# Second layer of a graph network: logits, maxima and aggregation run as one stage over blocks of 20 steps, in place of three stages

## The reference

```python
x = x * rsqrt(mean(x*x) + EPS) * rms_w @ W_down          # 3125 x 256, H = 4 heads of D = 64
xl = (x @ Wl).reshape(n, H, D);  xr = (x @ Wr).reshape(n, H, D)
msg = xl[src] + xr[dst]                                   # per edge, and one loop per node
e = einsum('ehd,hd->eh', leaky_relu(msg, 0.2), att)
m = segment_max(e, dst)
p = exp(e - m[dst]);  denom = segment_sum(p, dst)
out = segment_sum(p / (denom[dst] + 1e-16) * xl[src], dst) @ W_up
```

## Time and profile before

| what | value |
|---|---|
| median of 3 runs | 2532.44 us (2525.97 to 2538.17) |
| profiled execution: span, first to last instruction | 2193.8 us |
| profiled execution: its own total time | not recorded beside the span; the median lies 338.6 us above the span |
| busy, share of the span | PE 83%, DVE 69%, POOL 55%, ACT 45% |
| PE granted clock, mean | 0.95 |
| DMA | 537 MB, mean 245 GB/s |
| node stage, logits, between, aggregation, last stage | 217, 539, 30, 188.6, 109.2 us |

### The profile page before, as it was taken

How to read it: one execution, slowest core, us unless ns; L and a number is a source line. 1 busy time by engine, 2 the same in 40 slices (tenths; PEclk the granted TensorE clock), 3 DMA queues, 4 the chain that set the end, 5 groups by cost and what they waited for, 6 DMA issues and landing times. The chain is left out here.

```text
span 2193.8 us, 51473 instructions
## 1 busy us (share of the span) xinstructions
PE 1812.9 (83%) x12059; PEld 1247.6 (57%) x12060; DVE 1515.3 (69%) x3657; ACT 997.4 (45%) x3133; POOL 1196.8 (55%) x1696
## 2 busy tenths in 40 slices
PE   4899999995888888888849896887878878577788
PEld 3555555543566656665638774666666666456643
DVE  6577777747666666666669983554656556888867
ACT  3200000024777777777747662332333333566566
POOL 1122222223777777777711116777777776688780
PEclk9999999997999999999979998998999999698899
DMA  8344553313999999999999965887878877998657
GB/s 332 112 108 106 105 106 109 99 44 120 364 357 355 362 357 356 356 359 353 361 260 321 308 199 166 238 245 212 252 224 253 240 217 225 291 332 307 231 193 261
DMA packets 254654, 537.42 MB, mean 245 GB/s; under 512 B 40301, under 2 KB 146422, under 8 KB 254510
## 3 DMA queue, kind: packets, MB, share of 16 engines
q0 software_dynamic: 87696, 275.50, 36.7%
q1 hardware_dynamic: 72670, 174.80, 24.8%
q10 hardware_dynamic: 94176, 85.76, 13.6%
HBM read 447.61 MB, written 101.28 MB: 250 GB/s over the span
## 5 line engine op out<-in xcount | busy, mean ns | idle before, releaser
L1248 ACT ACTIVATE wone<-onehot,w 128x64 f32<-128x64 f32 x1760 | 432.3, 334 | 148.1 <-DVE onehot L1294 143.2
L161 POOL DMA_INDIRECT acc<-xl_table,csrc x392 | 395.8, 1010 | 127.3 <-issue 113.0
L1265 PE MATMUL banks<-w_sb,wone 128*64 128x256 f32 x2368 | 315.9, 392 | 80.5 <-DMA w_sb<-xp_table,isrc 54.8
L161 POOL DMA_INDIRECT w_sb<-xp_table,isrc x296 | 296.1, 1000 | 90.6 <-issue 55.5
L973 PE MATMUL banks<-w_sb,acc 128*128 128x512 f32 x736 | 342.6, 604 | 0.0
L1290 DVE TENSOR_TENSOR acc<-banks,acc 128x512 f32 x440 | 304.4, 692 | 0.0
L1737 PE MATMUL banks<-acc,onehot_t 128*128 x880 | 233.6, 410 | 85.0 <-ACT onehot_t L1712 62.6
L1765 DVE SCALAR_TENSOR_TENSOR prod<-banks,att_relu 128x1024 f32<-128x1024 f32 x110 | 134.7, 1224 | 206.3 <-ACT w L1702 203.4
L1737 PEld LDWEIGHTS banks<-acc,onehot_t 128*128 128x128 f32 x880 | 164.7, 196 | 148.0 <-issue 123.4
L1742 PE MATMUL banks<-acc,ident 128*128 x880 | 219.7, 394 | 20.4 <-POOL tabs L1664 20.3
L1265 PEld LDWEIGHTS banks<-w_sb,wone 128*64 128x64 f32 x2368 | 161.4, 136 | 130.5 <-issue 52.6
(11 more groups left out here) (340 smaller groups left out, 2951.8 us busy)
## 6 DMA issues: line engine op xcount, KB each, us to landing
edge_rows<-acc ACTq DMA_DIRECT2D x440, 128.0 KB
rows<-edge_rows SPq DMA_DIRECT2D x55, 1024.0 KB, 5.0
lt_bc<-local_dst ACTq DMA_DIRECT2D x110, 128.0 KB, 3.6
lt<-local_dst SPq DMA_DIRECT2D x110, 128.0 KB, 4.2
w<-acc SPq DMA_DIRECT2D x100, 128.0 KB, 3.7
x_table<-y POOLq DMA_DIRECT2D x25, 512.0 KB, 6.9
acc<-x_table SPq DMA_DIRECT2D x25, 512.0 KB, 3.7
low_bc<-src_low ACTq DMA_DIRECT2D x98, 128.0 KB, 4.2
```

The costliest lines, as they stand in the source:

```text
L161: return self.pool.indirect_dma_start(out, None, table, bass.IndirectOffsetOnAxis(ap=idx, axis=0), bounds_check=self.bound, oob_is_err=False)
L1248: last = nc.scalar.activation(wone[:, s, j, h, :], onehot[:, s, j, :], ACT.Copy, scale=w9[:, bass.ds(g * U + j, 1), h:h + 1].rearrange("p ...
L1265: nc.tensor.matmul(psum[WN * a:WN * (a + 1), j, k * C:(k + 1) * C], wone[:, s, j, h, :], slots[r][:, j, h * C:(h + 1) * C], start=True, st ...
```

## The change

The three parts named above become one Block. Work goes in blocks of 20 steps (5 groups; 22 blocks, and 2 more rounds to drain). One **turn** is one group of 4 steps, on every engine.

- POOL gathers rows per **step** (440 gathers by `isrc`, not 392 by `csrc`) into a ring of 15 groups, `ring`; `isrc` is first cut to its low 12 bits, so that no row is skipped. The rows stay in the ring until they are weighed, nine turns later. `edge_rows` and its stores and loads go.
- The node stage stores `xr` to HBM (`store_xr`, 25 transfers of 134 KB on SP). In the new stage SP loads, per group, 4 windows of 64 node rows (`near`, 67 KB each) and 2 broadcasts of window-local destinations, and per block 4 copies of the segment masks.
- PE: the one-hot products contract over 64 partitions, at partitions 0 and 64 in turn; one set of PSUM banks (0 to 3) for the logits, so that a group's products wait until DVE's product and ACT's copy have read the last. Sums go to banks 4 and 5, small matters to 6 and 7.
- Maxima run block by block; what has been summed in a window that goes over a block's border is rescaled (`rescale`).
- Weights: ACT takes 10 of a group's 16 head parts, DVE the other 6 in two instructions; POOL none. There is one `acc1`.
- Setup makes and stores the masks and window-local rows; `ldst` goes. The first layer's semaphores are cleared and freed at the node stage. In the last stage one addition a tile goes.

```diff
@@ node stage
+                    nc.vector.tensor_scalar(isrc[:], isrc[:], int(MISS) - 1, None, ALU.bitwise_and)
...
+                    def store_xr(t, s, m):
+                        sp.wait_ge(S["sf"], t + 1)
+                        sp.dma_start(xr_t[bass.ds(t * P, P), :], xr[:, bass.ds(t, 1), :].rearrange("p a n -> p (a n)"))\
+                          .then_inc(s_xrs, 16)
+                    pipelined(sp, NT, [(0, load_sums), (0, load), (0, load_down), (8, store_xr)],
...
+            nc.clear_and_free_semaphores(front_sems)
@@ the new stage; BG = 5, BS = 20, NBLK = 22, RG = 15, RU = 3, BACK = 10, BR = 80, ACT_HEADS = ACT_MORE = 2
+                def _(pool):
+                    for g in range(NG):
+                        gather.wait(s_wa, g - RG + 1)
+                        gather.wait(s_wd, g - RG + 1)
+                        for j in range(U):
+                            gather.rows_of(ring[:, g % RG * U + j, :], xl_t, isrc[:, g * U + j:g * U + j + 1])\
+                                  .then_inc(s_r[g % RG], 16)
...
+                    def load_near(g, s):
+                        wait(sp, s_pg, g - 2)
+                        at = windows.load(g)
+                        for j in range(U):
+                            half = slice(WN * (j // 2), WN * (j // 2 + 1))
+                            sp.dma_start(near[half, s, j % 2, :], xr_w[bass.ds(at[j], 1)].rearrange("w n c -> (w n) c"))\
+                              .then_inc(s_xr[s], 16)
...
+                    def logits(g, r, i, m):
+                        pe.wait_ge(s_ot, g + 1)
+                        pe.wait_ge(s_xr[rg % 3], 64 * (BG * m) + 64 * (rg // 3) + 64)
+                        wait(pe, s_pd, g)
+                        wait(pe, s_sc, g)
+                        for j in (0, 2, 1, 3):
+                            half = slice(WN * (j // 2), WN * (j // 2 + 1))
+                            nc.tensor.matmul(psum[:, j, 0:XRW], onehot_t[half, rg % 3, j % 2, :],
+                                             near[half, rg % 3, j % 2, :], start=True, stop=False)
+                        pe.wait_ge(s_r[rg], 16 * U * m + 16 * U)
+                        for j in range(U):
+                            last = nc.tensor.matmul(psum[:, j, 0:XLW], ident[:], ring[:, rg * U + j, :], start=False, stop=True)
+                        last.then_inc(s_pg, 1)
```

More of the change, by code:

```diff
@@ new lines, in gnn_kernel @@
+            in_wu = Words(accf, FREE, FREE2)
+            between = Words(accf, FREE2, NT * D - 2 * D)
+            in_xl = Words(accf, 0, NWP * P)
+            in_x1 = Words(accf, NT * D - 2 * D, NT * D)
+            ring = sb("ring6", [P, RG * U, XLW])
+            msg = in_w9.take(3 * U * H * HS).rearrange("p (s j h n) -> p s j h n", s=3, j=U, h=H)
+            near = in_xl.take(3 * 2 * XRW).rearrange("p (s q n) -> p s q n", s=3, q=2)
+            hsel, dsel, blk = (in_w9.take(n) for n in (H, BS, BR))
@@ new lines, in load_masks, with unit @@
+                    def load_masks(b, r):
+                        wait(sp, s_m, b - 2)
+                        for h in range(H):
+                            sp.dma_start(mask[h * BS:(h + 1) * BS, r].rearrange("p k e -> p (k e)"),
+                                         mask_t[bass.ds(b * BS, BS)].rearrange("s k e -> s (k e)")).then_inc(s_mk[r], 16)
+                    def unit(u, r, k, m):
+                        if k == 0:
+                            sp.dma_start(ends[0:TB], mask_t.rearrange("(b p) k e -> p b k e", b=NB)).then_inc(s_first, 16)
+                            with nc.allow_non_contiguous_dma(reason="the first edge of each block"):
+                                for h in range(H):
+                                    sp.dma_start(first16[h:h + 1, :],
+                                                 wloc_t.rearrange("(b s) e -> e b s", s=BS)[0:1, :, 0]).then_inc(s_first, 16)
+                        for i in range(BG):
+                            if k < NBLK:
+                                load_local(BG * u + i, (BG * r + i) % 3, None)
+                                load_near(BG * u + i, (BG * r + i) % 3)
+                            if i == 2 and k < NBLK:
+                                load_masks(u, r)
@@ L1903, in _ @@
+                    units(act, unit)
                 @block.tensor
                 def _(pe):
[L1905 to L1915 removed]
+                    pe.wait_ge(s_const, 2)
@@ new lines, in sums @@
+                    def sums(u, r, k, i):
+                        g, rg, on, r2, i2 = steps_of(u, r, k, i, BACK)
+                        if not on:
+                            return
+                        s = rg % 3
+                        pe.wait_ge(s_o, g + 1)
+                        pe.wait_ge(s_wa, g + 1)
+                        pe.wait_ge(s_wd, g + 1)
+                        for j in range(U):
+                            if j % 2 == 0:
+                                wait(pe, s_acc, (g - 1) * U + j + 2)
+                            for a in range(2):
+                                last = nc.tensor.matmul(sums_of(j)[WN * a:WN * (a + 1)], onehot[:, s, j, :],
@@ L1918, in group, with unit @@
                             last.then_inc(s_mm, 1)
-                    pipelined(pe, NG2, [(0, group)], 12, 12)
+                    def unit(u, r, k, m):
+                        for i in range(BG):
+                            if k < NBLK:
+                                logits(BG * u + i, r, i, m)
+                            if k == 0 and i == 3:
+                                borders()
+                            if 1 <= k <= NBLK:
+                                scan_step(u, r, k, i)
+                            sums(u, r, k, i)
@@ L1921, in _ @@
+                    units(pe, unit)
                 @block.vector
                 def _(dve):
[L1923 to L1929 removed]
@@ L1942, in _ @@
[L1942 to L1949 removed]
+                    windows = StepTiles(dve, wtab, "r1", U, NW)
@@ new lines, in unit @@
+                    def unit(u, r, k, m):
+                        for i in range(BG):
+                            g = BG * u + i
+                            back, _, adds, _, _ = steps_of(u, r, k, i, BACK)
+                            if adds:
+                                at = windows.load(back)
+                            if k < NBLK:
+                                product(g)
+                            if adds and i == 0 and k > 2:
+                                rescale(u, back, at[0])
+                            if k == 0 and i == 1:
+                                clear()
+                            if k == 0 and i == 2:
+                                row_borders()
+                            if k == 0 and i == 4:
+                                take_borders()
+                            if 1 <= k <= NBLK:
+                                scan_step(u, r, k, i, m)
+                            if adds:
+                                add(back, 0, at[0])
+                            if k < NBLK:
+                                reduce(g)
+                            if adds:
+                                add(back, 1, at[1])
+                            if k < NBLK:
+                                finish(g, r, i)
+                            if adds:
+                                add(back, 2, at[2])
+                            nodes(u, r, k, i)
+                            if adds:
+                                add(back, 3, at[3])
+                            weigh(u, r, k, i)
```

837 lines of the change are left out of this document (393 added, 444 removed).

## The result

The changed kernel takes 2560.97 us (median of 4 runs, 2554.42 to 2565.87) where the kernel before takes 2530.05 (4 runs, 2525.97 to 2538.17): ratio 1.0117, 95% interval 1.0082 to 1.0152. It is slower by 31 us; 2446 was forecast. About two thirds of the error hang on one sentence of the prediction: that 338.6 us lie outside the span.

The account below looks back on a forecast made before the run. It took POOL's gather issuing to bound the logits stage and DVE the aggregation. Fusing them at 5.7 us a turn gave 90 us less, `store_xr` 4 more: net -86, 2446 us, range 2400 to 2545.

Parts of the forecast that it names:

- Time outside the span: Whole execution: the median's 338.6 us above the profile's span of 2193.8 us were kept as a constant difference.
- First gather to last stage: New stage: start 11, first ten turns 53, a hundred turns 570, draining 34, together 668 us against 757.6.
- POOL: hidden: New stage: 440 gathers at 1.31 us, 5.24 us a turn, lie under the turn of 5.7 us.
- The signs that it named: New stage: among others DVE busy about 0.88, PE near 0.85; DVE idle over 80 us before small operations meant rival 3.
- rival 3: DVE's chain: nothing overlaps and each turn pays a 0.73 us hand-over, turn 6.7 us, 2557 us; chance 0.17.
- rival 1: PE's one-hot products: row halves don't pair, loop 6.05 us, mean turn 6.2 us, 2499 us; chance 0.22.
- A switch: PE, new stage: going from one product shape to another may empty the array, 0.2 us each, three a turn.
- the loop's 5.2: New stage, one set of logits banks: products, one switch, DVE's product, ACT's copy and hand-overs in sequence, 5.2 us.
- longer of the two: New stage: each turn costs the longer of DVE's work and the logits-bank loop, mean 5.7 us.
- Rival 2: POOL's gathers as floor: DVE operations overlap, switches cost nothing, turns of 5.24 us, 2399 us; chance 0.12.
- rival 4: ACT: table reloads at each change of function, 6.8 us in two turns a block, 2514 us; chance 0.04.
- Elsewhere: Outside the new stage: `store_xr` adds 0 to 13 us to the node stage, 4 taken; over 225 us there refutes it.

Follow-up runs that it names:

- e11: Changed kernel with the new stage's 440 indirect gathers replaced by plain transfers of the same size on POOL: 2284.53 us, kernel before 2539.93 on that chip.
- e3_one_scan: Changed kernel with three of the four scans of a block's scan step covering 8 columns instead of 128: 2118.77 us on the quick chip.
- e1: Changed kernel with one-hot products over all 128 rows of the array instead of its two halves: 2158.06 us on the quick chip.
- the bursts: PE products repeated to imitate a held-back PE: 38 bursts cost the kernel before 124 us, 37 cost the changed kernel 239 us.
- e2: Changed kernel with a step's four additions on DVE covering 8 columns instead of 264: 2121.27 us on the quick chip.

## Why the prediction was wrong

**Time outside the span: the step that failed.** It says "I keep that difference and apply the sum to both". The 338.6 us were no constant. They were time in two stages, 127 in one that the change leaves alone and 202 in one that it replaces; outside the span every run has 1.6 to 1.7 us. 338.6 is 13% of the median, and the prediction gives no reason why so much should lie outside. The other reading, that the profile wasn't of the timed kind, asked for a far wider range and a chance of slower near even. Of the 117 us between the net forecast (86 less) and the result (31 more), 39 come from the sum itself and 78 from this step, by the estimate that follows.

**What the change is worth when PE isn't held back.** First gather to last stage was put at 668 us. With e11's turn it is 15.5 to the first product (e3_one_scan: 1326.6 to 1342.1), 651 for 109 turns and 45 to the last stage (e11 and e3), 712. The turn is 5.97 against 5.7 forecast, inside the 5.3 to 6.0 that the prediction set as its test; the rest is the drain (45, not 34) and the start. With 1327 ahead and 108 behind, that is 2146 us against 2193, 47 less where 86 was forecast. An estimate, since the changed kernel itself didn't meet the quick chip; e1's measured 2158 against 2195 stands beside it. So by this estimate the direction was right for the profile that was read.

**Why it is slower on the usual chips.** From 712 to 988 us the new stage loses 276 us, the old ones 202; the 74 between turn 47 less into 28 more by the spans (31 by the medians). That the loss comes with the gathers is shown by e11. How the 74 come about is argued only: there are 440 gathers in place of 392, which at the old stage's 202/392 us a gather would be 25 of the 74, and the second aggregation, the same 218 us on the quick chip and on the usual ones, now runs beside gathers. What the bursts were to show, that one set of banks soaks up less, they don't. "POOL: hidden" was right for its own time and missed that its gathers act on PE; that is the second step that failed.

**The signs that it named.** On the usual chip the turn is 8.47 us, DVE is busy 0.58 of the stage and PE 0.60 where 0.88 and 0.85 were named (0.80 and 0.75 in e11). DVE's idle time before the additions is 85.3 us, over the 80 that were to speak for rival 3, but 48.9 of it is "remote", and in e3_one_scan it is 32.2.

**PE.** The eight half-height instructions take 1.16 us together where 1.2 was forecast, so rival 1 is refuted. A switch was priced at 0.2, three a turn; the identity product starts 1.09 us after the one-hots, and the first turn, without sums, takes 4.8 us against the loop's 5.2, so they cost next to nothing. That is also how far the Trainium skill's rule in "TensorEngine Tiling (Array Packing)", section "Key Properties", goes here: a drain by changing the mode isn't seen in these rows. A slip in the sum did no harm: PE's own 5.4 us is more than the loop's 5.2 and was left out of the longer of the two, and with it the mean turn is 5.7 as well.

**DVE.** The instructions came out about as costed: scans 0.40 to 0.48, additions 0.289. Small additions saved under half their cut, so DVE and loop seem about level, as the forecast's "longer of the two" has it. **Rival 3** gave 2557 us and the measurement 2561, by the wrong way: its 0.73 us hand-over in every turn would show on the quick chip too, and there turns are 5.7 to 6.1. **Rival 2** needed turns of 5.24; **rival 4** 44 table loads or more, and ACT has one in the stage. **Elsewhere**: the node stage stayed at 217 us, inside 225.

A term that was missing: five turns, each where the loop of 15 turns starts again, are 8.6 to 10.0 us long on the quick chip and in e11, where no hold covers them, 21 us of late products in all. Their cause wasn't tried, but the traces hold a sign of it: in e1, e2, e3 and e11 each of the five late products has two packets of 8 KB of an instruction queue (q14) landing 3.2 to 3.9 and 2.5 to 2.6 us ahead of it. That PE waits for its own instructions there is likely and not shown.

What stays open is what it is in a row of gathers that holds PE back, and why one chip is spared. Loading of instructions, an obvious suspect after the last paragraph, has no packet in the two holds shown (1484 to 1520.3 and 1761.3 to 1767.5 us in the changed kernel's trace), nor in about half of the other late products there. The Trainium skill, "DMA: Bandwidth & Descriptors", section "Terms", says that software on GpSimd writes the descriptors of its transfers into rings in SBUF. The traces list gathers and e11's plain transfers alike under the software queue, in equal number and size, and only gathers held PE back, so that route alone isn't the cause.

## What to carry to other kernels

Before any sum, hold the profile's span against the timed median; if they differ by much more than the 1.6 us seen here, get a trace of the timed kind, since which stage is longer decides what a change is worth. Where an idle engine is released by nothing that the trace shows, list what all other engines do in that time, over all runs: here one count pointed at indirect gathers, and one run without them settled it. Before an added load on an engine is read as time lost, look at the clock that it ran at: 26 of the 37 bursts in the changed kernel took up to twice as long as meant. A stage that is fused under gathers takes on what gathers do to the other engines, and a pause of 0.55 us between them can be worth more (170 us) than the fusion (an estimated 47).

## What the runs showed of the hardware

- On six of seven chips indirect gathers issued 0.30 us apart keep PE's completions back: up to 37 us in a row of 60, 3 to 8 us in rows of four. On one chip the same program shows none of it (573 against 700 us for 440 gathers in the same stage). In that time SyncE's issues are slow too, 13.6 us for four against 2.5; DVE's and ACT's instructions keep their lengths (DVE's product takes 1.22 us on either kind).
- A pause of 0.55 us between gathers shortens DVE's "remote" waits to 6.2 us at most and 103 us in all, from 42 and 301, and leaves their number (59, 58); one of 0.30 us, with or without a memset in it, does not.
- 34 half-height products take 6.9 us at a granted clock of 1.00 and 13.5 at 0.50.
- The mean granted clock of the new stage goes with the gathers: 0.79 with them, and 0.90 with plain transfers, at the same products on the same kind of chip:

```profile
1458.00:2180.00 722.00, 534.80 (x3839) 395.46 (x3840) 576.65 (x1603) 424.79 (x1640) 238.62 (x448) 0.90 0.53 143
```
